# Cross attention's probabilities split in halves on the query side and transposed by a DMA, in a decoder layer on one core

## The reference

```python
q = (xn @ w_q).reshape(B, SQ, NUM_HEADS, DIM_HEAD)
kv = context @ w_kv
k, v = jnp.split(kv, 2, axis=-1)
scores = jnp.einsum('bqhd,bkhd->bhqk', q * SCALE, k)
attn = jax.nn.softmax(scores, axis=-1)
out = jnp.einsum('bhqk,bkhd->bqhd', attn, v).reshape(B, SQ, INNER)
```

## Time and profile before

| | |
|---|---|
| median of 3 runs | 796.84 us (794.06 to 797.22) |
| the profiled execution | 791.3 us |
| its span, first to last instruction | 789.5 us, mean granted TensorE clock 0.892 |
| PE busy | 625.9 us (79%) |
| DVE busy | 521.6 us (66%) |
| ACT busy | 400.6 us (51%) |
| POOL busy | 218.5 us (28%) |

### The profile page before, as it was taken

How to read it: one execution, slowest core, us unless ns; L and a number is a source line. 1 busy time by engine, 2 the same in 40 slices (tenths; PEclk the granted TensorE clock), 3 DMA queues, 4 the chain that set the end, 5 groups by cost and what they waited for, 6 DMA issues and landing times. The chain is left out here.

```text
span 789.5 us, 14440 instructions
## 1 busy us (share of the span) xinstructions
PE 625.9 (79%) x4746; PEld 491.1 (62%) x4746; DVE 521.6 (66%) x1071; ACT 400.6 (51%) x973; POOL 218.5 (28%) x225
## 2 busy tenths in 40 slices
PE   4716678898888888888888888989768765789990
PEld 3615557677777767767767767867555452456660
DVE  3994357777777877876877777776848841953332
ACT  2435156566566466557556557445424612854341
POOL 3541021322232232232223123123212710233331
PEclk9965698999999999999999999999966986999995
DMA  9525200210210210110110110040216444533324
GB/s 236 192 71 167 64 1 2 65 54 1 66 53 0 63 53 0 52 61 3 39 51 27 23 67 27 12 134 28 87 49 239 145 146 131 181 60 60 62 28 106
DMA packets 58646, 57.35 MB, mean 73 GB/s; under 512 B 17266, under 2 KB 47986, under 8 KB 58610
## 3 DMA queue, kind: packets, MB, share of 16 engines
q1 hardware_dynamic: 54514, 51.68, 21.3%
q0 software_dynamic: 4096, 5.19, 4.1%
HBM read 46.74 MB, written 10.13 MB: 72 GB/s over the span
## 5 line engine op out<-in xcount | busy, mean ns | idle before, releaser
L633 POOL TENSOR_TENSOR probs<-probs,c_rcp 112x750 f32<-112x750 f32 x64 | 92.0, 1438 | 304.8 <-DVE c_rcp L995 304.8
L758 ACT ACTIVATE probs<-ps_s,c_neg 112x375 f32<-112x375 f32 x128 | 72.7, 581 | 24.1 <-DVE c_neg L987 24.1
L1313 PE MATMUL ps_t<-ident,probs 112*125 112x112 f32 x384 | 55.6, 282 | 19.5 <-DVE cpt_lo L999 19.5
L664 ACT ACTIVATE kt_hi<-ps_o 128x376 fp32r<-128x376 f32 x64 | 31.5, 493 | 74.1 <-PE ps_o L145 74.1
L1313 PEld LDWEIGHTS ps_t<-ident,probs 112*125 112x125 f32 x384 | 50.2, 194 | 26.3 <-issue 21.5
L143 PE MATMUL ps_o<-ctxt_hi,w_k_lo 128*128 128x376 f32 x128 | 49.0, 383 | 17.6 <-DVE oct_lo L873 17.1
L1621 POOL DMA_INDIRECT moe_sum<-gsh_hi,xs_in x21 | 33.5, 1595 | 103.8 <-ACT gsh_hi L1672 70.5
L985 DVE TENSOR_REDUCE c_max<-ps_s 112x2 f32<-112x750 f32 x64 | 59.4, 929 | 1.6 <-PE ps_s L145 1.6
L999 DVE SCALAR_TENSOR_TENSOR cpt_lo<-ps_t,cpt_hi 125x672 f16<-125x672 f32 x64 | 54.5, 851 | 8.2 <-ACT cpt_hi L765 8.2
L1941 PE MATMUL ps_h<-w_ex,xst_hi 128*128 (+1 forms) x168 | 58.8, 392 | 1.1 <-DVE xst_lo L1708 0.9
L750 ACT ACTIVATE v_hi<-ps_vx,v_scale 125x512 f16<-125x512 f32 x48 | 33.1, 689 | 35.2 <-PE ps_vx L145 35.2
(11 more groups left out here) (308 smaller groups left out, 1880.8 us busy)
## 6 DMA issues: line engine op xcount, KB each, us to landing
chunk<-in_L_ffn_ew_dram SPq DMA_DIRECT2D x24, 512.0 KB, 3.4
spare<-in_L_ffn_ew_dram SPq DMA_DIRECT2D x18, 512.0 KB
store<-in_L_ffn_ew_dram SPq DMA_DIRECT2D x6, 512.0 KB, 5.5
ctx_all<-in_ctx_dram SPq DMA_DIRECT2D x2, 1500.0 KB
ctx_raw<-in_ctx_dram SPq DMA_DIRECT2D x8, 375.0 KB
moe_in<-chunk SPq DMA_DIRECT2D x1, 2709.0 KB, 14.1
xs_in<-moe_in SPq DMA_DIRECT2D x21, 129.0 KB
plain_raw<-in_L_xattn_w_kv_dram SPq DMA_DIRECT2D x2, 1024.0 KB, 15.3
```

The costliest lines, as they stand in the source:

```text
L633: pool.tensor_tensor(p, p, r, ALU.mult).then_inc(sg["p_normed"], 1)
L758: act.activation(probs[:, s % 2, h, :], ps_s[0:N, h, 0:SK], ACT.Exp, bias=c_neg[:, s % 2, h:h + 1], scale=CROSS_SCALE, accum_out=c_sum[:, ...
L1313: last = pe.transpose(ps_t[0:SKT, h, t * N:(t + 1) * N], probs[:, s % 2, h, t * SKT:(t + 1) * SKT], ident[0:N, 0:N])
```

## The change

`rcp`, `p_transpose`, `cpt_hi`, `cpt_lo` and the banks `ps_t` go. POOL inverts the sums itself (a power of -1 and a product with the scale 2^14), and writes the high part of the probabilities in half precision to `p16`, on the query side. DVE subtracts it (`p_lo`, two instructions per step, in the place of `cpt_lo`, and for the pair of the step before, not of two steps before). One DMA per step, issued by SP, transposes the 112 x 1536 half-precision elements (two parts, two heads, 384 columns each) into `p16_t`. `pv` waits for that DMA. The keys are cut 128, 128 and 119 in place of three times 125. The keys' projection gets a bank of its own, `ps_kt`, and the two waits between it and `pv` go. SP's list is written anew around the transposes.

```diff
@@ attention_block
-        cpt = half_pair(nc, ctx, "cpt", [SKT, 2, ST, N])
+        p16 = sb("p16", [N, 2, 2, 2, PW], F16)
+        p16_t = sb("p16_t", [P, 2, 4 * ST, N], F16)
-        ps_t = ctx.enter_context(nc.psum_tensor("ps_t", [P, 2, 512], F32))
+        ps_kt = ctx.enter_context(nc.psum_tensor("ps_kt", [P, 512], F32))
@@ sync
+            def transpose_p(b, s):
+                n = PAIRS * b + s
+                sp.wait_ge(sg["p_lo"], n + 1)
+                if later(n - 1):
+                    sp.wait_ge(sg["pv_full"], n - 1)
+                sp.dma_start_transpose(p16_t[:, s % 2, :, :], p16[:, s % 2, :, :, :].rearrange("p a h n -> p (a h n)"))\
+                    .then_inc(sg[f"p_t{s % 2}"], 16)
+            load_ctx(0)
+            load_x(0)
...
+            shuffle(0)
+            load_ctx(1)
+            load_x(1)
+            load_chunk(0)
             for b in range(B):
-                entry(b)
+                more = b + 1 < B
+                for s in range(PAIRS):
+                    transpose_p(b, s)
+                    if more and s == 3:
+                        shuffle(b + 1)
+                    if more and s == 4:
+                        load_chunk(3 * b + 1)
+                    if b + 2 < B and s == 5:
+                        load_ctx(b + 2)
+                        load_x(b + 2)
+                    if more and s == 6:
+                        load_chunk(3 * b + 2)
+                    if b + 2 < B and s == 7:
+                        load_chunk(3 * b + 3)
+                    if not more and s >= 1 and 3 * (B - 1) + s - 1 < CHUNKS:
+                        load_chunk(3 * (B - 1) + s - 1)
@@ gpsimd
             def normalise(b, s):
+                pool.wait_ge(sg["c_exp"], 2 * (PAIRS * b + s) + 2)
...
+                pool.tensor_tensor(c_rcp[:, s % 2, :], c_sum[:, s % 2, :], neg_one[:, :], ALU.pow).then_inc(sg["c_rcp_part"], 1)
+                pool.wait_ge(sg["c_rcp_part"], PAIRS * b + s + 1)
+                pool.tensor_tensor(c_rcp[:, s % 2, :], c_rcp[:, s % 2, :], p_scale[:, :], ALU.mult).then_inc(sg["c_rcp_ready"], 1)
...
-                pool.tensor_tensor(p, p, r, ALU.mult).then_inc(sg["p_normed"], 1)
+                n = PAIRS * b + s
+                if later(n - 1):
+                    pool.wait_ge(sg[f"p_t{s % 2}"], 16 * (PAIRS // 2 * b + s // 2))
+                pool.tensor_tensor(p16[:, s % 2, 0, :, 0:SK], p, r, ALU.mult).then_inc(sg["p_normed"], 1)
@@ vector
-            def cpt_lo(b, s):
...
+            def p_lo(b, s):
+                dve.wait_ge(sg["p_normed"], PAIRS * b + s + 1)
+                for h in range(2):
+                    last = dve.scalar_tensor_tensor(p16[:, s % 2, 1, h, 0:SK], probs[:, s % 2, h, :], c_rcp[:, s % 2, h:h + 1],
+                                                    p16[:, s % 2, 0, h, 0:SK], op0=ALU.mult, op1=ALU.subtract)
+                last.then_inc(sg["p_lo"], 1)
+            def late_p_lo(b, s):
+                p_lo(*((b, s - 1) if s >= 1 else (b - 1, 7)))
@@ tensor, k_project and pv
-                if later(PAIRS * b + p - 4):
-                    pe.wait_ge(sg["oct_lo"], PAIRS * b + p - 4)
...
-                pe.wait_ge(sg["cpt_lo"], PAIRS * b + s + 1)
+                pe.wait_ge(sg[f"p_t{s % 2}"], 16 * (PAIRS // 2 * b + s // 2 + 1))
                 pe.wait_ge(sg["v_lo"], v_no("V02" if s < 4 else "V12", b))
-                pe.wait_ge(sg["kt_lo"], k_done)
```

More of the change, by code:

```diff
@@ L538, in _, with load_ctx @@
         def _(sp):
-            def entry(b):
+            def load_ctx(b):
                 if later(b):
@@ L588, in _ @@
             load_weights(sp, raw, A["sw1"], A["sw2"], A["sw3"], ffn_sg["raw_loaded0"])
-            for q in range(3 * (B - 2) + 2, CHUNKS):
-                load_chunk(q)
         @block.gpsimd
@@ L629, in normalise @@
             def normalise(b, s):
+                pool.wait_ge(sg["c_exp"], 2 * (PAIRS * b + s) + 2)
+                if later(PAIRS * b + s - 1):
+                    pool.wait_ge(sg["p_lo"], PAIRS * b + s - 1)
+                pool.tensor_tensor(c_rcp[:, s % 2, :], c_sum[:, s % 2, :], neg_one[:, :], ALU.pow).then_inc(sg["c_rcp_part"], 1)
+                pool.wait_ge(sg["c_rcp_part"], PAIRS * b + s + 1)
+                pool.tensor_tensor(c_rcp[:, s % 2, :], c_rcp[:, s % 2, :], p_scale[:, :], ALU.mult).then_inc(sg["c_rcp_ready"], 1)
                 pool.wait_ge(sg["c_rcp_ready"], PAIRS * b + s + 1)
@@ L749, in v_hi_cross @@
                     act.wait_ge(sg["v_scaling"], 9)
-                act.activation(v[0][:, q, t, :], ps_v[0:SKT, :], ACT.Copy, scale=v_scale[0:SKT, 0:1]).then_inc(sg["v_hi"], 1)
+                n = KEYS[t]
+                act.activation(v[0][0:n, q, t, :], ps_v[0:n, :], ACT.Copy, scale=v_scale[0:n, 0:1]).then_inc(sg["v_hi"], 1)
             def exps(b, s):
@@ L755, in exps @@
                 if later(PAIRS * b + s - 1):
-                    act.wait_ge(sg["t_full"], PAIRS * b + s - 1)
+                    act.wait_ge(sg["p_lo"], PAIRS * b + s - 1)
                 for h in range(2):
@@ L759, in exps @@
                                    scale=CROSS_SCALE, accum_out=c_sum[:, s % 2, h:h + 1]).then_inc(sg["c_exp"], 1)
-            def cpt_hi(b, s):
-                act.wait_ge(sg["t_full"], PAIRS * b + s + 1)
-                if later(PAIRS * b + s):
-                    act.wait_ge(sg["pv_full"], PAIRS * b + s)
-                act.activation(cpt[0][:, :, :, :].rearrange("p h t n -> p h (t n)"), ps_t[0:SKT, :, 0:ST * N], ACT.Copy,
-                               scale=P_SCALE).then_inc(sg["cpt_hi"], 1)
             def o_hi(b, s):
@@ L858, in iteration @@
                         place(3)
-                    if s >= 1:
-                        cpt_hi(b, s - 1)
-                    elif later(b):
-                        cpt_hi(b - 1, 7)
                     place(4)
@@ L865, in _ @@
             o_hi(B - 1, 6)
-            cpt_hi(B - 1, 7)
             o_hi(B - 1, 7)
@@ L1108, in iteration @@
                         place(0)
-                    if not lo_first and (s >= 2 or later(b)):
-                        late_cpt_lo(b, s)
+                    if not lo_first and (s >= 1 or later(b)):
+                        late_p_lo(b, s)
                     if s == 2:
                         place(1)
-                        rcp(b, s)
                     else:
@@ L1152, in iteration @@
                         chunk_max(3 * b + s - PAIRS + LATE)
+            dve.wait_ge(sg["padded"], 3)
             iterations(dve, iteration)
-            cpt_lo(B - 1, 6)
+            p_lo(B - 1, 7)
             o_lo(B - 1, 6)
-            cpt_lo(B - 1, 7)
             o_lo(B - 1, 7)
@@ L1288, in v_project @@
                     pe.wait_ge(sg["v_lo"], v_no(f, b) - 1)
-                rows = slice(t * SKT, (t + 1) * SKT)
+                rows = slice(t * P, t * P + KEYS[t])
                 for k in range(KD):
-                    last = product(pe, ps_v[0:SKT, :], tuple(c[:, k, rows] for c in ctxt),
+                    last = product(pe, ps_v[0:KEYS[t], :], tuple(c[:, k, rows] for c in ctxt),
                                    tuple(w[:, k, 512 * q:512 * q + 512] for w in w_v), start=k == 0, stop=k == KD - 1)
@@ L1305, in scores, with pv @@
                 last.then_inc(sg["s_full"], 1)
-            def p_transpose(b, s):
-                pe.wait_ge(sg["p_normed"], PAIRS * b + s + 1)
-                if later(PAIRS * b + s):
-                    pe.wait_ge(sg["cpt_lo"], PAIRS * b + s)
-                for h in range(2):
-                    for t in range(ST):
-                        last = pe.transpose(ps_t[0:SKT, h, t * N:(t + 1) * N],
-                                            probs[:, s % 2, h, t * SKT:(t + 1) * SKT], ident[0:N, 0:N])
-                last.then_inc(sg["t_full"], 1)
-            def pv(b, s, k_done):
-                pe.wait_ge(sg["cpt_lo"], PAIRS * b + s + 1)
+            def pv(b, s):
+                pe.wait_ge(sg[f"p_t{s % 2}"], 16 * (PAIRS // 2 * b + s // 2 + 1))
                 pe.wait_ge(sg["v_lo"], v_no("V02" if s < 4 else "V12", b))
-                pe.wait_ge(sg["kt_lo"], k_done)
                 if later(PAIRS * b + s):
@@ L1393, in place @@
                                 fill(b + 1, f)
-                    k_done = PAIRS * b + min(s + 3, PAIRS if not more else s + 3)
                     scores(b, s)
```

65 lines of the change are left out of this document (25 added, 40 removed).

## The result

The changed kernel takes 814.65 us (median of 4 runs, 812.79 to 817.84), the kernel before 795.45 (4 runs, 790.5 to 797.22): a ratio of 1.0256, interval 1.0196 to 1.0315. The forecast was 823 us, slower, with 790 to 862 as its range.

A forecast was written before the change was run, and what follows sets the result against it. It saw a weave of three engines, each waiting a little, with chunk loads pacing the last entry. Losses from SP's order, net of small gains, sum to 7.4 + 12X = 26.6 us, giving 823 us on the median, range 790 to 862.

The forecast's parts named there:

- X: SP's list: how much later the next DMA lands behind a transpose; taken as 1.6 us, ends 0.4 and 3.7.
- (3): Last entry: chunk loads wait behind maxima, low part and transpose in each round; costs 6 + 5X us.
- (1): Steps 4 and 5: `o_shuffle` behind the transpose makes the rows late, without cover; 0.2 + X an entry, 1.4 + 7X in all.
- (2): Step 7's chunk load, issued behind a transpose: free up to X = 1.8, beyond it each entry pays the difference.
- (4): Gate and shared expert loads come after the last transpose; some 8 us of work hides them, uncovered up to 6 us.
- (a): Steps 0 to 4: gain left from PE's dropped transposes and `oct_lo` waits; 0.8 us an entry, ends 0 and 6.1.
- (b): DVE's low part takes 1.15 us; POOL's power and product delay probabilities about 1 us, costing 0.5 in step 1.
- (c): After PE takes the rows in step 5: no probability transposes in the chain, so no gain, 0.15 us of loss.
- The clock: Left out of the sum: PE idling longer may be granted the lower clock, as in steps 2 and 7.
- PE's freed time is the entry's time: Faster rival: PE's saved work and waits shorten each entry; 786 us, or 751 with all 11.2 us; chance 0.19.
- The last entry alone: Slower rival: the self attention's rows are off the chain, only the last entry loses; 811 us, chance 0.13.
- Transposes slower than the steps: Slower rival: transposing DMAs over 7.7 us set the pace; 1097 us at 12 us each, chance 0.06.

The follow-up runs named there:

- e1: Changed kernel with only the self attention's `o_shuffle` issued ahead of the transpose of its step in SP's list; 805.9 us, 1.0168.
- e2: Changed kernel with only the chunk loads of step 6 and of the last entry issued ahead of the transpose; 791.1 us, 0.9983.
- e3: Changed kernel with both `o_shuffle` and those chunk loads issued ahead of the transpose in SP's list; 782.0 us, 0.9857.
- e5: Kernel before, with SP waiting for `cpt_lo` ahead of `o_shuffle` and the last entry's chunk loads, no transposing DMA; 797.6 us, 1.0060.
- e10: Changed kernel with POOL keeping the power and DVE only waiting for the exponentials at the reciprocal's old places; 829.2 us, 1.0453.
- e4: Changed kernel with the keys' projection back in the outputs' bank, with its two waits; 822.6 us, 1.0379.
- e9: Kernel e3 with POOL computing the power of the sums twice, first into an unused buffer; 791.8 us, 0.9991.
- e7: Changed kernel with the reciprocal back on DVE in its old places, POOL keeping the product with the scale; 846.5 us, 1.0672.
- e12: Kernel e3 plus DVE's step 5 low parts of rows and context ahead of the probabilities', and six unused PE transposes in step 3; 771.4 us, 0.9749.

## Why the prediction was right, and where its steps were off

It was right on the sign and 8 us too high, and the mechanism that it named, SP's late DMAs, is the one that e1, e2 and e3 show. That the number came so close is in part luck: at the measured X of 2.0 its sum has 15.4 us for the entries 0 to 6 and 16 for the last, and measured are 4.5 and 15.8, the second by two errors that cancel. Taken by its own steps:

**X, the transpose ahead of the next DMA.** Taken as 1.6, measured as 2.0: 1.40 us from the transpose's issue to that of `o_shuffle`, and 0.6 us more from that to `o_rows` (3.46 against 2.83 in the earlier trace rows). The sum 7.4 + 12X would then be 31.4, or 823 us against the profiled execution's own 815.3. The two ends held. By the figure of the Trainium skill, in "Advanced Engine Details and Errata", section "X-Bar Transpose (TRN2)", an estimate of the whole transpose was 1.0 us; the trace has 1.36 us for the issue alone and 3.5 to landing. So the bandwidth alone does not give the price.

**(3), the last entry.** Predicted 6 + 5X, 14 at 1.6 and 16 at 2.0; measured 15.8. Its rounds had 7.5 + X = 9.5 and 6.3 + X = 8.3 us; the steps took 8.43 and 10.00, then 8.01 and 8.47. This is the term that e2 tests, and where the loss is: 10.8 of its 15.8 us went when the loads were put first. The sum agrees better than its parts. The four rounds up to the last maxima grew by 13.5 us where 14.9 were booked (the fifth ends behind them), and the steps 0 to 2 lost 2.3 us, where 2 were taken off as won: 0.8 by the low part in step 0, and 1.5 in step 2, which was granted 0.85 in place of 1.00.

**(1), the late rows.** The wait is there, 25.5 us in eight, 1.9 to 4.3 each where 2 to 3 were predicted. Its price was too high, and this is the term that was mis-sized: 3.0 us an entry before the gain is taken off (0.85 + X and the 0.15), 21 in seven, where undoing it gave 8.7 (e1). The step that failed is "so there is no cover", taken for every entry. It holds where step 4 runs at the full clock, as in the earlier trace rows. There `ot_lo` comes 10.1 to 10.2 us after the maxima of step 4, and in e1 7.7: 2.4 us late, near the 0.85 + X. But only two of the seven steps 4 were such. Where step 4 took some 6.6 us, `ot_lo` came at 9.9 and in e1 at 9.0 to 9.2, and where it took 7.4 at 9.95 in both. Twice 2.4 and four times some 0.8 are 8.0 us, an estimate from these times, and entries 0 to 6 of e1 are 7.9 shorter. e5 has the same: 0.4 to 0.5 us at the full clock, nothing beside a longer step 4.

**(2), step 7's chunk.** Free up to X = 1.8, it said; at 2.0 the chunk comes 0.2 us late, and step 7 grew by 0.25. But the wait there hid a gain of the clock: with the chunk in time (e3) step 7 takes 7.59 us at a granted 1.00 in most entries, and so it does in the kernel before where it is granted 1.00 (e5, 7.57 us), in place of 9.13 at 0.89.

**(4)** The 1.1 us behind the last maxima bound it; no run was made for it.

**(a), the gain up to step 4.** 0.8 us taken, 1.8 measured by the table. Step 0's loss of 0.47 is the lateness that I had put in step 1 (0.5). Step 1 gave 1.13 where 0.85 was left, and for another reason: DVE's wait for the exponentials went (with it back, e10 has 5.69 us), and not PE's for `oct_lo` (e4). Step 3 gave nothing. Step 2, booked at nothing, gave 1.09; but it was granted 0.86 before and 0.97 in the mean after, and e5 shows the kernel before taking 10.7 us at 1.00, less than the 11.1 of the changed kernel there. So the clock, which the sum left out, accounts for the 1.09 by itself, and no run shows that the transposes that went gave anything there. It also made most of the 1.80 us that DVE waits for PE in the earlier trace rows.

**(b), the low part and POOL.** Two instructions take 1.12 us back to back, taken as 1.15. The power is 0.73 us and not 0.55, the product 0.20 and not 0.36: 0.93 together, against 0.91. e9 shows that such a delay costs where the low part comes first, as the step said, at 0.47 and 0.65 us for 0.73. The step failed by what it left out: that DVE no longer waits for the exponentials (e7, e10). It had the low part of step 6 covered, which holds (e9), and left out the last entry's.

**(c), nothing gained after the rows.** This failed: step 6 fell by 1.19 us in every entry. The cast and the low part of the layer norm's output were no longer held up beside POOL; they took 0.77 and 0.40 us less, nearly all of the 1.19 (last section). The granted clock is not the reason: step 6 takes 6.95 us at 1.00 too in the kernel before (e5) and 5.76 at 0.70 in e12. The prediction named both effects as outside its sum, and as possible losses only.

**The clock** cost 1.0 us an entry in step 4 (6.28 against 5.28, with entries of 5.18 at full clock among them) and gave back the 1.09 of step 2. Over entries 0 to 6 the mean granted clock fell from 0.94 to 0.89.

**The rivals.** *PE's freed time is the entry's time*, 786 us: SP's order did hide a gain, and e3 shows it, 2.2 us an entry (413.6 against 428.7), short of the 6.1 to 11.2 of that rival and of the 3.8 at which it decides. It is not shown to be PE's freed time either: the steps that are shorter are 1 (DVE's wait), 6 (POOL out of the way), 2 and 7 (the clock). *The last entry alone*, 811 us, was nearest to the number (3.7 off against 8.3), yet for the wrong reason: e1 shows that the rows do cost 8.7 us, which gains elsewhere made up for. *Transposes slower than the steps*: a transpose lands in 3.5 us, well inside a step. The estimate of 15.7 us by the other page of the Trainium skill, "VectorE: DVE Perf Modes", section "The three transpose paths", falls with it: twelve squares in one DMA are not twelve times one.

## What to carry to other kernels

A DMA that waits for late data must not stand in a queue ahead of one that is ready and urgent: the same DMAs in another order of issue made 32 us of 815 here, more than the whole loss. An engine that stands in its queue for a small result holds up all that is queued behind it: moving DVE's reciprocal to POOL was worth 32 us here, and the bare wait 14.5. A wait read from one execution can be the clock's: DVE's 1.80 us for PE were 0.27 in another execution, with the same work at the full clock. After every change of order look at the granted clock by stretches before reading a step as longer or shorter, since a step may take 5.2 or 6.6 us with the same work in it.
